# Attention output turned in 32x32 blocks by VectorE instead of by TensorE, with a projection in four row tiles

## What is computed

```
qkv = relu(x @ qkv_weight.T)                      # q, k, v; 32 heads of 8 channels
vk   = einsum('bnhe,bnhd->bhed', [v, 1], k)       # per sequence and head
vk_q = einsum('bhed,bnhd->bnhe', vk, q)
att  = vk_q[..., :8] / (vk_q[..., 8:] + 1e-15)    # 'att', tokens x 256
x1 = layernorm(x + att @ proj_weight.T + proj_bias)
h  = silu(x1 @ wg.T) * (x1 @ wu.T)                # 768 hidden, weights int / 127
out = layernorm(x1 + h @ wd.T)
```

## Time and profile before

| What | Value |
|---|---|
| Median of three runs | 555.05 us (554.89 to 556.29) |
| The profiled execution | 556.24 us, of which the span of the trace is 554.4 us |
| TensorE (PE) busy | 542.7 us, 98% of the span, 3275 matmuls |
| VectorE (DVE) busy | 387.2 us, 70% |
| ScalarE (ACT) busy | 221.3 us, 40% |
| GpSimd (POOL) busy | 80.2 us, 14% |
| Granted TensorE clock, mean | 0.995 |

### The profile page before, as it was taken

One profiled execution on the slowest core, in us unless ns is written; L12 is line 12 of the kernel. 1 busy time (PEld: TensorE's weight loads), 2 busy tenths in 40 slices (PEclk: granted clock), 3 DMA queues, 4 the chain that ended last, 5 costly groups with the idle time before them and its releaser, 6 DMA issues.

```text
span 554.4 us, 8767 instructions
## 1 busy us (share of the span) xinstructions
PE 542.7 (98%) x3275; PEld 480.0 (87%) x3275; DVE 387.2 (70%) x867; ACT 221.3 (40%) x376; POOL 80.2 (14%) x94
## 2 busy tenths in 40 slices
PE   8889999999999999999999999999999999999995
PEld 5778989898898988989898898988989898898975
DVE  5786758486684957758487684957858587684976
ACT  3356243543524445243542524445243442524431
POOL 1011110011110111110011110111110011100212
PEclk9999999999999999999999999999999999999999
DMA  8300121201111030121202112030121202102001
GB/s 302 154 0 2 39 77 40 76 0 76 38 38 76 0 113 0 38 76 38 76 0 76 38 38 76 0 113 1 38 76 38 76 0 76 38 0 77 2 39 38
DMA packets 8652, 29.02 MB, mean 52 GB/s; under 512 B 960, under 2 KB 1728, under 8 KB 8640
## 3 DMA queue, kind: packets, MB, share of 16 engines
q1 hardware_dynamic: 8640, 28.85, 14.4%
HBM read 20.46 MB, written 8.39 MB: 52 GB/s over the span
## 4 chain that ended last, share of the span: by engine, by line
PE 91%; DVE 4%; DMA 2%; ACT 1%; issue 1%; POOL 0%; SPq 0%; POOLq 0%
PE abcd_ps L580 48%; PE gate_ps L580 17%; PE up_ps L580 16%; PE abcd_ps L616 6%; PE abcd_ps L624 5%; DMA wg_raw<-w_gate 1%; DMA xT_raw<-x_chan 1%; DVE x1T_lo L336 0%; DVE h L343 0%; DVE xT_lo L336 0%; ACT silu L240 0%; DVE wg_lo L336 0%; DVE st L562 0%; DVE st L397 0%; DVE r L558 0%
## 5 line engine op out<-in xcount | busy, mean ns | idle before, releaser
L343 DVE SCALAR_TENSOR_TENSOR h<-up_ps,silu 128x512 f32<-128x512 f32 x96 | 66.0, 687 | 82.7 <-ACT silu L240 82.7
L240 ACT ACTIVATE silu<-gate_ps 128x512 f32<-128x512 f32 x96 | 57.4, 598 | 107.3 <-PE gate_ps L580 107.3
L580 PE MATMUL abcd_ps<-wd_hi,h_hi 128*128 128x256 f32 x384 | 93.1, 283 | 0.8 <-DVE h_lo L336 0.8
L580 PE MATMUL abcd_ps<-wd_hi,h_lo 128*128 128x256 f32 x384 | 92.9, 283 | 0.0
L580 PE MATMUL gate_ps<-x1T_hi,wg_hi 128*128 128x512 f32 x192 | 79.6, 415 | 2.0 <-DVE x1T_lo L336 1.9
L336 DVE TENSOR_TENSOR h_lo<-h,h_hi 128x512 fp32r<-128x512 f32 x96 | 65.9, 686 | 14.3 <-ACT h_hi L235 11.2
L580 PE MATMUL up_ps<-x1T_hi,wu_hi 128*128 128x512 f32 x192 | 75.7, 394 | 0.0
L580 PE MATMUL up_ps<-x1T_lo,wu_hi 128*128 128x512 f32 x192 | 75.6, 394 | 0.0
L580 PE MATMUL gate_ps<-x1T_lo,wg_hi 128*128 128x512 f32 x192 | 75.3, 392 | 0.0
L580 PEld LDWEIGHTS abcd_ps<-wd_hi,h_hi 128*128 128x128 f32 x384 | 73.7, 192 | 1.1 <-DVE h_lo L336 1.0
L580 PEld LDWEIGHTS abcd_ps<-wd_hi,h_lo 128*128 128x128 f32 x384 | 73.7, 192 | 0.0
(11 more groups left out here) (118 smaller groups left out, 968.9 us busy)
## 6 DMA issues: line engine op xcount, KB each, us to landing
x_raw<-x_tok SPq DMA_DIRECT2D x16, 512.0 KB, 3.3
xT_raw<-x_chan SPq DMA_DIRECT2D x15, 512.0 KB, 3.2
out<-out_sb SPq DMA_DIRECT2D x15, 512.0 KB, 2.6
wg_raw<-w_gate SPq DMA_DIRECT2D x1, 768.0 KB, 6.8
wu_raw<-w_up SPq DMA_DIRECT2D x1, 768.0 KB, 8.2
wd_raw<-w_down SPq DMA_DIRECT2D x1, 768.0 KB, 9.6
xT_raw<-x_chan SPq DMA_DIRECT2D x2, 256.0 KB, 3.4
wkv_raw<-w_kv SPq DMA_DIRECT2D x1, 512.0 KB, 5.1
```

The source lines that it names most:

```text
L240: nc.scalar.activation(silu[:, j % 2, :], gate_ps[j % 2][:], ACT.Silu, scale=WSCALE).then_inc(silu_ok[j], 1)
L343: nc.vector.scalar_tensor_tensor(out=h[:, j, :], in0=up_ps[j % 2][:], scalar=WSCALE, in1=silu[:, j % 2, :], op0=ALU.mult, op1=ALU.mult).th ...
L580: last = mm(dst, lhsT, rhs, start=start and n == 0, stop=stop and n == len(pairs) - 1)
```

## The change

`attT_of` is gone. VectorE turns `att` with one instruction that transposes every 32x32 square (`att_squares`), into memory of the gate weights' raw form, which is free by then. A square lies where its 32 tokens came from, so the 256 channels lie in NCB = 8 groups of 32 on each of four partition groups of 32 (NG = 4), and each partition group holds other tokens. The projection runs as 8 x 3 x 4 = 96 matmuls with 32 channels each, on four row tiles of the array (`tile_position`); row tile g writes bank g of the four. The weights are laid on all four partition groups, by eight DMAs of 128 KB, and rounded on ScalarE. `q_relu` writes q so that the tokens end up in their old places. Since the projection takes all four banks, the down product moves to `gate_ps[1]` and `up_ps[1]`, with waits on `h_ok[5]` and `r2_ok`. `h` has three buffers, and some tiles and semaphores share memory; the FFN's arithmetic is the same. The `att_squares` of a step stands between h of hidden blocks 2 and 3.

The diff, cut to its core:

```
-        wp_hi, wp_lo = sb("wp_hi", [P, KC, C], FP32R), sb("wp_lo", [P, KC, C], FP32R)
+        wp_hi, wp_lo = sb("wp_hi", [P, NCB, C], FP32R), sb("wp_lo", [P, NCB, C], FP32R)
...
+        down_ps = (gate_ps[1][:], up_ps[1][:])
...
-            sp.dma_start(wp_raw[:], proj_w).then_inc(wp_in, 16)
+            for g in range(NG):
+                for k in range(KC):
+                    sp.dma_start(wp_raw[g * SQ:(g + 1) * SQ, k * NG:(k + 1) * NG, :],
+                                 proj_w[:, k, :].rearrange("(j s) n -> s j n", s=SQ)).then_inc(wp_in, 16)
             load_xT(1)
             sp.dma_start(wg_raw[:], gate_w).then_inc(wg_in, 16)
...
-                    relu(dst[:, k, :], banks[k], q_ok[k])
+
+                    relu(dst[:, k, :].rearrange("p (t g s) -> p g t s", t=NT, g=NG),
+                         banks[k].rearrange("p (g t s) -> p g t s", g=NG, t=NT), q_ok[k])
...
             def attT_hi_of(b):
-                T_hi_of(b, attT_mm, attT_hi, attT_hi_ok, (A, B))
+                act.wait_ge(att_sq_ok, b + 1)
+                for k in range(KC):
+                    half = slice(k * NG, (k + 1) * NG)
+                    rounded(attT_hi[:, half, :].rearrange("p c n -> p (c n)"),
+                            att_sq[:, half].rearrange("p c t s -> p (c t s)"), attT_hi_ok[k])
...
             q_relu(0, dst=qT_first)
+            act.wait_ge(wp_in, 16 * NG * KC)
+            rounded(wp_hi[:], wp_raw[:], wp_hi_ok)
             for t in range(NT):
                 kv_relu(t, 0, (A, B)[t % 2])
...
+            def att_squares(b):
+                dve.wait_ge(att_ok, b + 1)
+                if not isinstance(b, int) or b > 0:
+                    dve.wait_ge(attT_hi_ok[KC - 1], b)
+                nc.vector.transpose(att_sq.rearrange("p c t s -> p t c s"),
+                                    att[:].rearrange("p t (c s) -> p t c s", s=SQ)).then_inc(att_sq_ok, 1)
...
-            rounded(wp_hi[:], wp_raw[:], w_hi_ok, 0)
-            minus_hi(wp_lo[:], wp_raw[:], wp_hi[:]).then_inc(wp_lo_ok, 1)
+            dve.wait_ge(wp_hi_ok, 1)
+            minus_hi(wp_lo[:, :NG], wp_raw[:, :NG], wp_hi[:, :NG])
...
             def proj_of(b):
-                pe.wait_ge(attT_lo_ok[KC - 1], b + 1)
-                for t in range(NT):
-                    tok = slice(t * P, (t + 1) * P)
-                    last = add_up((CC, D)[t // 2][:, (t % 2) * C:(t % 2 + 1) * C], [p for c in range(KC) for p in (
-                        (attT_lo[:, c, tok], wp_hi[:, c, :]),
-                        (attT_hi[:, c, tok], wp_hi[:, c, :]),
-                        (attT_hi[:, c, tok], wp_lo[:, c, :]))])
-                    if t % 2:
-                        last.then_inc(proj_mm[t // 2], 1)
+
+                for c in range(NCB):
+                    if c % NG == 0:
+                        pe.wait_ge(attT_lo_ok[c // NG], b + 1)
+                    for n, (part, w) in enumerate(((attT_lo, wp_hi), (attT_hi, wp_hi), (attT_hi, wp_lo))):
+                        for g in range(NG):
+                            rows = slice(g * SQ, (g + 1) * SQ)
+                            last = mm(abcd[:, g, 0:C], part[rows, c, :], w[rows, c, :],
+                                      start=c == 0 and n == 0, stop=c == NCB - 1 and n == 2, tile_position=(g * SQ, 0))
+                            if c == NCB - 1 and n == 2 and g % 2:
+                                last.then_inc(proj_mm[g // 2], 1)
...
+                    if j == 1 and (not isinstance(b, int) or b > 0):
+                        pe.wait_ge(r2_ok[0], b)
+                        pe.wait_ge(r2_ok[1], b)
...
             def down_of(b, tiles=range(NT)):
+                pe.wait_ge(h_ok[NH - 1], b + 1)
...
-                q_of(i + 1, free=r1_ok)
+                pe.wait_ge(r1_ok[1], i + 1)
+                q_of(i + 1)
...
             proj_of(0)
 
+            pe.wait_ge(r1_ok[0], 1)
             vk_of(1)
```

More of the change, by code:

```diff
@@ L23 @@
 NH = HID // P
+SQ = 32
+NG, NCB = P // SQ, C // SQ
+HS = 3
 BANK = 512
@@ L76, in build @@
         xb = sb("xb", [P, NT * C])
-        qT, qT_first = sb("qT", [P, KC, TB]), sb("qT_first", [P, KC, TB])
+        qT = sb("qT", [P, KC, TB])
+        qT_first = silu = sb("silu", [P, 2, TB])
         kv = sb("kv", [P, NT, 2 * KC, VW])
@@ L129, in build @@
         rstd1_pair, x1_pair = signals("rstd1_pair", 2), signals("x1_pair", 2)
-        down_tile, r2_tile, st2_tile = signals("down_tile", NT), signals("r2_tile", NT), signals("st2_tile", NT)
-        mv2_tile, ve2_tile = signals("mv2_tile", NT), signals("ve2_tile", NT)
-        rstd2_tile, out_tile = signals("rstd2_tile", NT), signals("out_tile", NT)
+        down_tile, r2_tile, st2_tile, mv2_tile, ve2_tile, rstd2_tile, out_tile = (
+            signal(f"{n}_tile") for n in ("down", "r2", "st2", "mv2", "ve2", "rstd2", "out"))
         last_down = [bank[:, :C] for bank in (A, B, CC, D)]
@@ L342, in h_of @@
                     dve.wait_ge(up_mm[j], b + 1)
+                    if j >= HS:
+                        dve.wait_ge(h_lo_ok[j - HS], b + 1)
+                    elif not isinstance(b, int) or b > 0:
+                        dve.wait_ge(h_lo_ok[j + HS], b)
                     nc.vector.scalar_tensor_tensor(
-                        out=h[:, j, :], in0=up_ps[j % 2][:], scalar=WSCALE, in1=silu[:, j % 2, :],
+                        out=h[:, j % HS, :], in0=up_ps[j % 2][:], scalar=WSCALE, in1=silu[:, j % 2, :],
                         op0=ALU.mult, op1=ALU.mult).then_inc(h_ok[j], 1)
@@ L424, in r2_add @@
                 nc.vector.scalar_tensor_tensor(
-                    out=pair(r2, n), in0=(A, B)[n], scalar=WSCALE, in1=pair(x1_of_b, n), op0=ALU.mult, op1=ALU.add).then_inc(r2_ok[n], 1)
+                    out=pair(r2, n), in0=down_ps[n], scalar=WSCALE, in1=pair(x1_of_b, n), op0=ALU.mult, op1=ALU.add).then_inc(r2_ok[n], 1)
             def normed(dst, r, mv, rs, ok, tiles=range(NT)):
@@ L680, in down_of @@
             def down_of(b, tiles=range(NT)):
+                pe.wait_ge(h_ok[NH - 1], b + 1)
                 for t in tiles:
-                    last = down_part(b, t, range(NH), (A, B)[t // 2][:, (t % 2) * C:(t % 2 + 1) * C])
+                    last = down_part(b, t, range(NH), down_ps[t // 2][:, (t % 2) * C:(t % 2 + 1) * C])
                     if t % 2:
@@ L791, in _ @@
             gate_up(i, *range(NH))
-            pe.wait_ge(r2_ok[1], i)
             for t in range(2):
```

95 lines of the change are left out of this document (53 added, 42 removed).

## The result

The changed kernel takes 562.92 us (median of four runs, 562.34 to 563.41), the kernel before 554.97 us beside it (554.56 to 556.29): 1.0139 times as long, with a 95% interval of 1.0119 to 1.0158. The forecast was 559.1 us with a range of 550 to 600. The profiled execution spans 561.2 us, against 554.4 before. Executions of before come in two kinds: of 38 others that ran beside the experiments, 30 had a mean granted clock of 0.997 to 0.999 and spanned 552.4 to 553.7 us, and 8 had 0.995 or 0.996 and spanned 553.9 to 555.1; the recorded one is of the second kind (0.995). So the two traces differ by 6.8 us and the medians by 8.0.

The account below looks back on a forecast made before the run. TensorE, busy for 98% of the span, was taken to bound the kernel. Start +5.1, loop -1.4 and last block +0.35 gave +4.05 us on the profiled 556.24, so 560.3; against the median 559.1 us, range 550 to 600.

Parts of the forecast that it names:

- Part 1: Loop step, TensorE: the eight transposes of att go, a gross gain of 0.88 us per step.
- Part 2: Gate and up of hidden block 4: TensorE waits for h of block 2, leaving 0.40 us of gain per step.
- Part 3: Squares on VectorE take 1.12 us; h of block 3 keeps 0.2 us of slack, so they cost nothing.
- Part 4: Projection: four row tiles run at once, 0.120 us per group, sum unchanged at 2.88 us.
- C: Projection rival: starting is the limit, 0.20 us per group, 590 us; chance 0.14 with in-between values.
- Rival B: Projection: row tiles do not run at once, up to 4 x 0.120 us per group, about 697 us; chance 0.14.
- Part 5: Projection's ends: entering and leaving the tiled mode costs 0.30 us per block.
- Part 6: Start: weights land at about 12.6 us, TensorE's next matmul comes +3.5 us, clock +1.6 us; start +5.1 us.
- Part 7: Last block: the residual sum's halves both end with the last matmul, losing the gain made ahead; +0.35 us.
- D: Rival: start costs little, weights as early as now, no clock loss, free switches; 550 us, chance 0.14.
- E: Rival: squares take 2.2 us, h of block 3 is 0.9 us late in each step; 573 us, chance 0.08.

Follow-up runs that it names:

- best version: The both repaired kernel with the squares of att turned in two halves of four channel blocks: 549.0 us, ratio to before 0.989.
- loop 1: Changed kernel with h of hidden block 2 computed between the second and third product of att, no longer after the fourth: 563.08 us.
- the first experiment: The same run as loop 1: changed kernel with only h of hidden block 2 computed earlier, 563.08 us.
- loop 2: The loop 1 kernel with h of block 3 also computed earlier, ahead of the squares, in blocks 1 to 15: 558.94 us.
- the squares in two halves: The same run as best version: the both repaired kernel with the squares of att turned in two halves, 549.0 us.
- both repaired: Changed kernel with loop 2's order, projection weights in one 1 MB transfer behind wg, their rounding on ScalarE and VectorE later: 551.72 us, ratio to before 0.9932.

## Why the prediction was right, and where its sizes were off

The direction was right, and the time missed by 3.8 us. Trace against trace the parts of the miss are: start +1.7, loop +1.0, and 1.1 because I took off the 1.2 us by which the profiled execution of before lay above its median, while that of the changed kernel lay on its own (563.03 against 562.92). The first and the third belong together: the low clock of the recorded before makes its start look dearer by 1.6 us. Against an execution without it the start was put at 5.1 us and cost 8.4, which is 3.3 too little; with the loop's 1.0 that is 4.3, and the remaining half microsecond is not traced. The range from 550 to 600 us was wide enough to hold all of this.

- **Part 1** (0.88 us of transposes): right. The best version's 0.51 us a step is this less the two changes of mode.
- **Part 2** (0.40 us left behind the wait for h of block 2): right in the trace, 0.41. What I did not draw from it is that h of block 3 stood 0.28 us behind as the next wait, so that taking the first away gives nothing, as loop 1 showed. Part 3 even had that slack, at 0.2 us; I forgot my own number when I wrote the first experiment.
- **Part 3** (squares 1.12 us, no cost): 1.235 us each, and no cost as long as h of block 2 is late anyway. With h of block 2 early they held up h of block 3 (0.62 us in front of block 5 in loop 1); with both early they cost 0.17 us a step, until halved.
- **Part 4** (a group in 0.120 us): right, against C and against the Trainium skill's 3.07 times (TensorE: Matmul & The Clock Gate, section on packing small matmuls), 4 times for 256 columns here, 3.07 for 512 there; no run tries 512. The weight loads of a group overlap too: the four in loop 2's last line took 0.19 us together, what one alone takes. Rival B needed matmuls of different row tiles to queue; 24 in a row on one tile do queue, and give 795 us and not 697, since the clock falls as well.
- **Part 5** (0.30 us per block): mis-sized, 0.39 to 0.40, twice measured. A step gave 0.03 us where -0.40 + 0.30 promised 0.10, and over 14 steps that is the 1.0 us.
- **Part 6** (start +5.1): the mechanism was right, link for link, and its first number wrong. The landing was put at 12.6 us by bytes over 347 GB/s; it was 15.7, because transfers to 32 partitions move at 205. With the rate of whole-partition transfers the landing was 12.6, TensorE's next matmul 15.07 where the text had 15.3, and the time 560. So the pause cost 6.3 us (11.86 to 18.16) where the sum had 3.5. The clock's share, put at 1.6 us, was 2.4 in the changed kernel's trace and 1.4 to 2.5 in the others, so that term was right within what executions differ by. The eight matmuls that it was worked out from came from the very stretch of before that, by their mean clock, most of its executions do not have.
- **Part 7** (last block +0.35): right. From `vk_of(15)` to the last FFN's first matmul the shift grew from 6.45 to 6.82 us; that matmul came at 530.79 before and at 537.61 now.
- **D and E** did not happen; E's wait, for h of block 3, comes already with squares of 1.25 us (loop 1), once h of block 2 is out of the way.

## What to carry to other kernels

When work leaves the bound engine, follow every wait behind the one that takes its place: here three stood one behind the other (h of block 2, h of block 3, `attT_lo`). The first repair alone brought nothing, the second 0.32 us a step, the third another 0.16. Small matmuls on different row tiles give back the full factor if neighbours in the stream are on different tiles, and each visit to the tiled mode costs 0.4 us, so collect them. A layout that writes to 32 partitions at a time halves its load's rate, which cost 3 us here; a load and its rounding that stand ahead of what the bound engine waits for cost 7 us in all, as much as the change earns in its steps at best (14 times 0.51).

## What the runs showed of the hardware that I had not expected

- Eight transfers to 32 partitions each moved 203 to 219 GB/s with the DMA engines' busy share at 1.05 to 1.17 in 10 to 14 us; eight to 128 partitions moved 353 to 434 at 1.04 and 1.06. The busy share doesn't show it, only the GB/s beside it do.
- TensorE's granted clock went from 1.00 to 0.50 inside a stretch without any pause, while it ran one row tile of 32 rows at a time. With four tiles at once, 2.9 us in 33, it stayed at 1.00; no run keeps four tiles going for as long as that one did.
- The granted clock fell near 40 us in some recordings and not in others: before was at 0.60 in 40 to 44 us, the squares in two halves at 0.63, both repaired, with the same start, at 1.00. It costs some 1.5 us, which is about what the 8 of 38 executions of before with the lower mean clock took longer.
- A matmul of 32 rows and one of 128 rows have the same pitch, 0.120 us for 256 columns.
- Two transposes of 128x512 on VectorE took 1.29 us together against 1.235 us for one of 128x1024: halving costs 0.05 us.
